# Key and image-key weights without the 64 columns of padding, in a fused cross-attention kernel

## What is computed

```python
q = split_heads(x @ w_q)
k, v = split_heads(text @ w_k), split_heads(text @ w_v)
out_text = softmax(q k^T / 4) v
k_ip, v_ip = split_heads(ip @ w_k_ip), split_heads(ip @ w_v_ip)
out_ip = softmax(q k_ip^T / 4 + mask(bbox)) v_ip
out = (merge(out_text) + merge(out_ip)) @ w_out + b_out + x
```

## Time and profile before

| | |
|---|---|
| median of three runs | 210.18 us (210.06 to 210.33) |
| profiled execution | 210.0 us, of which the span of the trace 208.2 us |
| mean granted clock of PE | 0.982 of full speed |
| busy PE, DVE, ACT, POOL | 182.1, 147.8, 129.3, 103.9 us |
| loads and stores | 37.72 MB in 35814 packets |
| `wk`, four loads | 192.0 KB each |
| `wk_ip`, one load | 768.0 KB, 8.1 us from issue to landing |

### The profile page before, as it was taken

The page is one execution under the profiler, slowest core; times in us unless marked ns, Lnnn a source line. Parts: engine busy times, 40 slices in busy tenths (PEclk is TensorE's granted clock), DMA queues, the critical chain, the costliest instruction groups (busy, mean ns, idle before and its releaser), DMA issues.

```text
span 208.2 us, 4662 instructions
## 1 busy us (share of the span) xinstructions
PE 182.1 (87%) x1608; PEld 148.4 (71%) x1608; DVE 147.8 (71%) x355; ACT 129.3 (62%) x298; POOL 103.9 (50%) x107
## 2 busy tenths in 40 slices
PE   0895999999967989999989999999999978998971
PEld 0775999999965648777666958676795946766741
DVE  1668562366827687877968797978779799778482
ACT  4529363342337967955794797389378749849640
POOL 7004029601360758655683786577376546638200
PEclk9999599999999999999999999999999999999999
DMA  5999798899982575784785756578754772220301
GB/s 146 274 404 359 268 341 192 191 241 295 226 201 77 136 176 131 239 190 112 203 241 145 227 164 191 127 214 274 164 159 134 232 160 84 63 74 0 100 30 63
DMA packets 35814, 37.72 MB, mean 181 GB/s; under 512 B 11216, under 2 KB 34000, under 8 KB 35792
## 3 DMA queue, kind: packets, MB, share of 16 engines
q1 hardware_dynamic: 35792, 37.44, 63.8%
HBM read 25.63 MB, written 11.47 MB: 178 GB/s over the span
## 4 chain that ended last, share of the span: by engine, by line
PE 32%; SPq 18%; DVE 17%; DMA 15%; ACT 8%; issue 6%; POOL 3%; DVEq 0%; ACTq 0%; POOLq 0%
PE bank L420 20%; SPq L298 8%; DVE negmax L1049 6%; DMA x_raw<-xT 4%; DMA raw<-wk_ip 4%; SPq L316 4%; DMA vr<-vip_dram 3%; PE bank L570 3%; ACT raw L826 3%; PE bank L584 3%; PE bank L492 3%; PE bank L525 2%; DVE pip L973 2%; DMA q_dram<-q_l 2%; DVE q_l L973 2%
## 5 line engine op out<-in xcount | busy, mean ns | idle before, releaser
L1049 DVE TENSOR_REDUCE negmax<-bank 128x4 f32<-128x448 f32 x80 | 49.9, 623 | 22.5 <-PE bank L492 22.0
L826 ACT ACTIVATE raw<-bank 112x512 f32<-112x512 f32 x80 | 46.4, 599 | 2.9 <-PE bank L525 1.6
L1199 POOL TENSOR_TENSOR x_l<-x_raw,x_h 128x768 fp32r<-128x768 f32 x8 | 15.3, 1916 | 20.5 <-ACT x_h L763 20.5
L570 PE MATMUL bank<-raw,v 112*32 112x256 f32 x320 | 22.2, 385 | 1.2 <-DVE late L1095 0.4
L1250 POOL TENSOR_TENSOR late<-late 128x256 f32<-128x256 f32 x20 | 14.7, 733 | 17.0 <-DVE late L1095 17.0
L584 PE MATMUL bank<-raw,con 112*32 112x256 f32 x320 | 22.1, 382 | 0.0
L420 PE MATMUL bank<-ctx_hl,key_w 128*128 128x448 f32 x72 | 16.9, 398 | 5.8 <-DVE ctx_hl L973 5.8
L420 PE MATMUL bank<-wo_h,ctx_hl 128*128 128x320 f32 x80 | 19.8, 317 | 2.4 <-DVE ctx_hl L973 2.4
L1199 POOL TENSOR_TENSOR ctx_hl<-late,ctx_hl 128x256 fp32r<-128x256 f32 x20 | 14.7, 737 | 13.7 <-ACT ctx_hl L853 10.2
L492 PE MATMUL bank<-key_w 96*128 96x240 f32 x80 | 17.1, 305 | 4.6 <-DVE ips L1052 1.9
L868 ACT ACTIVATE log_z<-bank 128x256 f32<-128x256 f32 x24 | 9.2, 384 | 17.7 <-PE bank L584 17.5
(11 more groups left out here) (103 smaller groups left out, 463.6 us busy)
## 6 DMA issues: line engine op xcount, KB each, us to landing
x_raw<-xT SPq DMA_DIRECT2D x8, 384.0 KB, 4.4
q_dram<-q_h SPq DMA_DIRECT2D x8, 384.0 KB, 3.8
q_dram<-q_l SPq DMA_DIRECT2D x8, 384.0 KB, 3.5
late<-x SPq DMA_DIRECT2D x8, 320.0 KB, 3.4
out<-late SPq DMA_DIRECT2D x8, 320.0 KB, 2.5
qs<-q_dram SPq DMA_DIRECT2D x12, 192.0 KB, 3.4
k_dram<-late SPq DMA_DIRECT2D x4, 480.0 KB, 3.9
key_w<-q_dram SPq DMA_DIRECT2D x9, 192.0 KB, 3.5
```

The costliest lines, as they stand in the source:

```text
L570: mm = pe.matmul(oz_bank[(k + c) % 2][32 * j:32 * j + 32, 0:S], v[k][:, 2 * p + ab, :], probs[:, p, S * ab:S * ab + S], start=n < 4, stop= ...
L826: nc.scalar.activation(probs[:, p, :], b_banks(b)[p % len(b_banks(b))][0:TEXT, :], ACT.Exp, scale=SCALE).then_inc(p_done, 1)
L1049: nc.vector.tensor_reduce(negmax[:, t, :, 2 * g:2 * g + 2].rearrange("p a q -> p q a"), s[:, :, 0:TEXT].rearrange("p (q a) n -> p q a n", ...
L1199: sub = lambda o, a, b: nc.gpsimd.tensor_tensor(o, a, b, ALU.subtract)
```

## The change

The host no longer pads `wk` and `wk_ip`; the loads carry 320 columns a chunk instead of 384, the splits of both work on 320, and the third block of key products uses 64 weight columns and writes 64 output partitions. Tiles keep their size, so a row of `w_raw` now takes four separate pieces of 1280 bytes for `wk_ip` instead of one of 6144. The count of instructions on the engines stays as it was.

```diff
-            splits.append((wk_ctx_in[j], 32, wk_h[:, j, :], wk_l[:, j, :], w_raw[:, 0, j, :]))
+            splits.append((wk_ctx_in[j], 32, wk_h[:, j, 0:D], wk_l[:, j, 0:D], w_raw[:, 0, j, 0:D]))
...
-        splits.append((kip_in, 32, wkip_h[:], wkip_l[:], w_raw[:, 1]))
+        splits.append((kip_in, 32, *(t[:, :, 0:D] for t in (wkip_h, wkip_l, w_raw[:, 1]))))
...
+        def key_cols(m):
+            return slice(m * P, min((m + 1) * P, D))
+        def key_rows(m):
+            return slice(0, min(P, D - m * P))
...
-                sp.dma_start(w_raw[:, 0, j, :], wk[:, j, :]).then_inc(wk_ctx_in[j], 16)
+                sp.dma_start(w_raw[:, 0, j, 0:D], wk[:, j, :]).then_inc(wk_ctx_in[j], 16)
...
-            sp.dma_start(w_raw[:, 1], wk_ip).then_inc(kip_in, 16)
+            sp.dma_start(w_raw[:, 1, :, 0:D], wk_ip).then_inc(kip_in, 16)
...
-                    mm = three(ip_key_bank[:, 64 * m:64 * m + 64],
-                               [(w[:, j, m * P:(m + 1) * P], t[:, j, 0:B * IP]) for j in range(CC)
+                    mm = three(ip_key_bank[key_rows(m), 64 * m:64 * m + 64],
+                               [(w[:, j, key_cols(m)], t[:, j, 0:B * IP]) for j in range(CC)
...
-                        w_hi, w_lo = (w[:, j, m * P:(m + 1) * P] for w in (wk_h, wk_l))
+                        w_hi, w_lo = (w[:, j, key_cols(m)] for w in (wk_h, wk_l))
...
-                        mm = three(bank[2 * m + half][:, 0:448],
+                        mm = three(bank[2 * m + half][key_rows(m), 0:448],
...
-        "wk": by_chunk(padded(wk)),
+        "wk": by_chunk(wk),
...
-        "wk_ip": by_chunk(padded(wk_ip)),
+        "wk_ip": by_chunk(wk_ip),
```

More of the change, by code:

```diff
@@ L768, in high_keys @@
                 act.wait_ge(k_ready, n)
-                copy(kc_h[m][:, 4 * half:4 * half + 4, 0:TEXT],
-                     bank[2 * m + half][:, 0:448].rearrange("p (b n) -> p b n", b=4)).then_inc(kh_done, 1)
+                r = key_rows(m)
+                copy(kc_h[m][r, 4 * half:4 * half + 4, 0:TEXT],
+                     bank[2 * m + half][r, 0:448].rearrange("p (b n) -> p b n", b=4)).then_inc(kh_done, 1)
             def high_image_keys():
@@ L774, in high_image_keys @@
                 for m in range(XC):
-                    ins = copy(kc_h[m][:, :, TEXT:KEYS],
-                               ip_key_bank[:, 64 * m:64 * m + 64].rearrange("p (n b) -> p b n", b=B))
+                    r = key_rows(m)
+                    ins = copy(kc_h[m][r, :, TEXT:KEYS],
+                               ip_key_bank[r, 64 * m:64 * m + 64].rearrange("p (n b) -> p b n", b=B))
                 ins.then_inc(kh_done, 1)
@@ L984, in low_keys @@
                 dve.wait_ge(kh_done, n)
-                sub(kc_l[m][:, b4, 0:TEXT], bank[2 * m + half][:, 0:448].rearrange("p (b n) -> p b n", b=4),
-                    kc_h[m][:, b4, 0:TEXT]).then_inc(kl_done, 1)
+                r = key_rows(m)
+                sub(kc_l[m][r, b4, 0:TEXT], bank[2 * m + half][r, 0:448].rearrange("p (b n) -> p b n", b=4),
+                    kc_h[m][r, b4, 0:TEXT]).then_inc(kl_done, 1)
             def low_image_keys():
@@ L990, in low_image_keys @@
                 for m in range(XC):
-                    ins = sub(kc_l[m][:, :, TEXT:KEYS], ip_key_bank[:, 64 * m:64 * m + 64].rearrange("p (n b) -> p b n", b=B),
-                              kc_h[m][:, :, TEXT:KEYS])
+                    r = key_rows(m)
+                    ins = sub(kc_l[m][r, :, TEXT:KEYS], ip_key_bank[r, 64 * m:64 * m + 64].rearrange("p (n b) -> p b n", b=B),
+                              kc_h[m][r, :, TEXT:KEYS])
                 ins.then_inc(kl_done, 1)
```

## The result

The changed kernel takes 206.94 us (median), the kernel before 210.12 in the same comparison: ratio 0.9858, 95% interval 0.9824 to 0.9892. The forecast, 207.8 against 210.18, is a ratio of 0.989. A ratio leaves out executions over 1.5% above the fastest of their kernel; in the third comparison these are three of the changed kernel's six, and with all executions the medians there, 207.81 and 209.31, have a ratio of 0.993. The profiled execution took 206.71 us, its span 204.9.

What follows compares the result with a forecast made beforehand. The last-ending chain bounds the kernel: the `wk_ip` load, its splits, then PE without a gap to 39.5. Queries end 2.4 us sooner: 210.0 - 2.4 = 207.6, plus 0.18 for the median, 207.8; range 205.8 to 209.3.

Steps and rivals of the forecast that it cites:

- The landing: Prologue load of `wk_ip`: lands 0 to 0.64 us sooner, 0.3 taken, from the bytes of `wk` alone.
- The byte account: Prologue loads: `wk` saves 0.32 us at best; `wk_ip` gives its saved bytes back in packets, 1.92 against 1.93 us.
- The splits: ACT's cast and DVE's subtraction of `wk_ip`, between landing and PE: 0.19 + 0.29 = 0.48 us saved.
- The first key projection: PE ahead of the image keys: no gain counted; the 2.81 us wait before 17.99 covers a late end.
- The start: PE's image keys begin at 17.21 instead of 17.99, by 0.30 from the landing and 0.48 from the splits.
- The narrow products: Last 12 image key products: 0.075 us each at full clock, 0.15 at half; bounds 0.055 and 0.11.
- The clock: Granted PE clock falls to half at 20.02 as before and returns 3.0 us after the first query product.
- signs that I had named as showing the prediction wrong: Unchanged `wk_ip` landing and narrow spacing; clock back after the queries; `vr` still landing at 58.9; a second half-clock stretch.
- late return: Rival: clock returns near 26.84, all 24 query products run at half clock; 1.3 us gained, 208.9; chance 0.24.
- Width changes: Rival: changing weight width stalls PE 0.08 us each, 0.64 in the second key projection; 208.5; chance 0.05.
- Behind it: After the queries: key stores, key reads, query store and `vr` all shift by about 2.3 us; loop time unfixed.
- Absorbed: Rival: the queue's backlog sets the landing of `vr`, so the loop starts when it did; 210.2; chance 0.08.

Runs made afterwards that it cites:

- e1: Changed kernel with the padded loads and splits put back, so only the narrow products remain; ratio 0.991 to the kernel before.
- e6: Kernel before with image key products of 128 moving columns instead of 64, nothing else; ratio 0.988 to the kernel before.
- e8: Narrow products with padded loads and splits, plus 128 moving columns in the image keys; ratio 0.991 to the kernel before.
- e2: Changed loads and splits alone, 128 weight columns kept in every product with the padding zeroed once on POOL; ratio 0.991 to the kernel before.
- e3: Changed kernel with image key products of 128 moving columns instead of 64; ratio 0.987 to the kernel before.
- e5: Changed kernel measured again, nothing altered; ratio 0.989 to the kernel before.
- e7: Changed loads and splits, 128 weight columns in every product, 128 moving columns in the image keys; ratio 0.988 to the kernel before.
- e9: e3 with loads of output weights and bias deferred until the first key and query reads are issued; ratio 1.000 to the kernel before.
- e10: e3 measured again, nothing altered; ratio 0.995 to the kernel before.
- e12: Changed kernel measured a third time, nothing altered; ratio 0.987 to the kernel before.
- e11: e9 with the boxes' load put behind `wq` and their masks later on DVE; ratio 0.995 to the kernel before.

## Why the prediction was right, step by step

**The landing: too small, and not one number.** I forecast 13.74, that is 7.8 us after the issue, with 0 to 0.64 us of gain. The changed kernel's three profiles have 6.6, 7.2 and 7.2. Over all profiles, the four kernels with padded loads (before, e1, e6, e8) average 7.85, the eight with the changed loads 7.21 (6.6, 7.5, 6.7, 7.2, 7.3, 8.6, 6.6, 7.2, from the changed kernel, e2, e3, e5, e7, e9, e10, e12): 0.64 sooner, at the edge of my bounds, with a scatter of over 1 us inside either group.

Most of the scatter sits in a load that the change does not touch. The boxes, 64 KB, are issued at 4.98, ahead of the image context and of `wk_ip`. The view of the tile `box`, in the kernel before and in the changed one:

```profile
L278 SPq DMA_DIRECT2D box<-bbox x1: 432/432/432, 5.0 to 5.0; - x1
...
DMA to landing us min/median/max: 6.5/6.5/6.5
```
```profile
L286 SPq DMA_DIRECT2D box<-bbox x1: 432/432/432, 5.0 to 5.0; - x1
...
DMA to landing us min/median/max: 4.7/4.7/4.7
```

In the five of these twelve profiles in which the boxes landed 6.0 us or more after their issue (before, e2, e6, e8, e9) `wk_ip` took 7.5 to 8.6 us; in the seven others, e1 with its padded load among them, 6.6 to 7.3. And in e11, where the boxes are issued behind `wq`, it took 5.8, the least of all fourteen. So most of the 1.5 us between the first two profiles goes with the boxes and is not shown to be the change's. What is the change's shows on the `wk` loads ahead of the boxes: the median of the four lands 3.7 to 4.0 us after the issue with padding and 3.1 to 3.4 without, with no overlap. By the packet records of the two traces (65 ns for 1536 bytes, 55 for 1280, 234 for 6144) `wk` saves 512 x 10 / 16 = 0.32 us and `wk_ip` 0.11, together 0.43 instead of my 0.3. The byte account was right in direction and nearly in size; the rest of the first profile's earlier landing is not in it.

**The splits: right.** 0.21 and 0.27 measured, 0.19 and 0.29 forecast.

**The first key projection: a cover that was used up.** I counted it at nothing because PE waited 2.81 us behind it. In the first profile it took 10.32 us instead of 9.35, and the wait was gone. It cost nothing yet: DVE's split ended at 14.35 + 1.50 = 15.85, and PE began 0.14 us behind such an end before (17.99 against 16.08 + 1.77), so the weights too would have let it begin at 15.99. In e5 and e12 waits of 0.54 and 1.69 were left. The projection's length changes because its first products start 0.373 us apart, 16 of the 36 in this profile and 10 in the kernel before, and the later ones about 0.20. 448 columns at 1.2 GHz take 0.373 us, although the granted clock of these stretches reads 1.00. So how much of an earlier landing counts depends on how long that projection takes.

**The start: 17.21 forecast; 15.99, 16.56 and 16.63 measured.** The term was too small, for the landing's reason: most of what was missing goes with the boxes, which the prediction left out.

**The narrow products: right, at the lower bound.** I took 0.075 and 0.15 from a transposing product with twice the moving columns; 0.057 and 0.107 were measured, which is my lower bound of 0.055 at full clock. The weight load bounds them: half the weight columns take half the time, and in e3 twice the moving columns take no longer.

**The clock.** This step was wrong. The fall came in all three profiles of the changed kernel, earlier than forecast (18.54, 18.63 and 19.65 against 20.02). The return 3.0 us after the first query product did not hold: 5.3 us in the first profile, 4.4 in e5, 2.8 in e12. What the rows show in its place is the length of the stretch at half clock, 6.8 us before, in the first profile and in e5, and 3.4 in e12, wherever the queries lay. Two of the signs that I had named as showing the prediction wrong came true: in the first profile the clock returned behind the queries (25.36 against 25.34), and a second stretch at half clock stood in e12 and, from 168.8 to 172.2, in e5. The first profile is the rival *late return*, but with an earlier start it cost no more than the forecast had left room for.

In the sum, the start gave 2.00 instead of 0.78, the image keys 1.75 instead of 1.5, the queries took back 1.03 instead of nothing: 2.72 instead of 2.4. Of the 1.75, 1.28 is the twelve narrow products, 12 x (0.213 - 0.107); the rest comes from the fall, which came 2.55 us after the image keys' start instead of 2.03. The total was right partly because two errors went opposite ways, and that is luck. So is part of the first comparison's 3.2 us: the other two ratios stand for 2.2 and 2.8. I had taken 0.2% for what a measurement of this kernel can tell; the intervals reach 0.3 to 0.8% to either side.

**Width changes: no stall.** The second key projection, with eight changes of width, takes 7.34 us against 7.42. In e5 and e12 it takes 7.33 and 7.32. The rule that a change of tiling mode drains TensorE (the Trainium skill, TensorEngine Tiling (Array Packing), Key Properties) cannot be seen in these rows; if this change of width is one of mode, its drain is under what they resolve.

**Behind it: right.** DVE's second context was ready 2.2 us ahead of need. The query store came at 42.51 (42.9 forecast), `vr` at 49.26 (49.3), POOL at 55.91 (56.6). The lead of 2.72 us was 2.36 at the issue of `vr` and 3.06 at POOL: `vr` landed after 6.58 us instead of 7.29. Over the fourteen profiles POOL begins 6.65 to 7.35 us behind the issue of `vr`, and these two happen to be the ends of that range, so 0.7 of the 3.3 us of span is luck again. *Absorbed* as I had put it, with `vr` landing at 58.9 all the same, did not happen. e3 shows another place where it begins: a second key projection 2.5 us sooner yet is worth 0.7 at the first scores. In e5 and e12 too the chain that ended last runs through the key stores and query reads in DRAM, and in e12 PE waits 0.36 us for them.

What stays open: how the gain, 1.1 to 1.4% by the three ratios, divides between loads and products in the mean of many executions, since e1, e2, e6, e7 and e8 overlap; why the boxes land so far apart, and whether the change brings them forward; and what decides when the clock falls and returns in a given execution.

## What to carry to other kernels

Padding in a weight that is multiplied by few moving columns costs full price: with 64 or 128 of them the weight load set the pace here, so half the weight columns took half the time, while under 448 moving columns the same padding cost next to nothing on TensorE (7.42 us against 7.34). Look for such products on the path first. And before a difference of a few microseconds between two profiles is explained, look at how far one load lands apart in two executions of the same kernel: here it was over a microsecond, more than three times the 0.3 us that I had forecast for that load, and most of it came from another load ahead of it in the queue.

## What the runs showed of the hardware

- The same padded load of 768 KB landed 7.0 to 8.2 us after its issue in four executions. The load of the boxes, 64 KB issued 0.95 us ahead of it, landed 4.0 to 7.1 us after its issue in twelve, and the larger load behind it took 7.5 to 8.6 us where the boxes took 6.0 or more, and 6.6 to 7.3 elsewhere.
- The granted clock fell to half behind products of 64 moving columns without any wait of PE (changed kernel, at 18.54), and behind products of 128 moving columns after a wait of 2.73 us (e6, at 20.6). It stayed at half for 3.4 us in e12 and for 6.8 us in the changed kernel's first profile.
- A product of 64 weight columns and 64 moving ones takes 0.057 us at full clock and 0.107 at half; one of 64 weight columns and 128 moving ones takes 0.06 at full clock (e3).
- With the clock held throughout the prologue the time did not follow: e11's profile shows it at 1.00 from 15 to 28 us, and the ratio was 0.995, no lower than the changed kernel's.
